# Four-layer kernel, last phase: finished rows stored to the output at once, spline parts placed by three engines and added there by accumulating transfers

## The reference, cut to what matters

```
tile_idx = argmax over the tiles of the chosen cluster
x_slice = xf[token, the 8 features of tile_idx]
tile_min, tile_max = min, max of x_slice over all tokens with that tile
u  = clip((x_slice - mn) / (mx - mn + 1e-08), 0.0, 1.0 - 1e-06)
gi = clip((u * GRID).astype(int32), 0, GRID - 1)
delta = (bases[tile,j,gi] + slopes[tile,j,gi] * (u - gi/GRID)*GRID) * output_scale[tile]
out = x + (zeros with delta at the tile's 8 features)
```

## Time and profile before

| | us |
|---|---|
| median of three runs | 7930.12 |
| the profiled execution's own time | 7928.37 |
| span of its trace | 7926.6 |
| core phase's last instruction on DVE ends | 7681.5 |
| first instruction of the chunks on DVE | 7771.65 |
| last DVE instruction | 7921.9 |

### The profile page before, as it was taken

The page is one execution under the profiler, slowest core; times in us unless marked ns, Lnnn a source line. Parts: engine busy times, 40 slices in busy tenths (PEclk is TensorE's granted clock), DMA queues, the critical chain, the costliest instruction groups (busy, mean ns, idle before and its releaser), DMA issues. The chain is left out here.

```text
span 7926.6 us, 217947 instructions
## 1 busy us (share of the span) xinstructions
PE 7123.9 (90%) x74510; PEld 5211.8 (66%) x74510; DVE 6564.5 (83%) x7897; ACT 4860.3 (61%) x11212; POOL 5927.2 (75%) x3528
## 2 busy tenths in 40 slices
PE   8799999999999999999999999899999997888864
PEld 4577777777777777777777777644444443555542
DVE  7799999999999999999999999822322324999976
ACT  7778878878878877878878877611111112555530
POOL 1499999999999999999999999800000002999964
PEclk9999999999999999999999999999999998999975
DMA  5500000000000000000000000022222112333325
GB/s 209 165 0 17 17 0 17 17 0 17 17 0 17 17 0 17 17 0 17 17 0 17 17 0 6 37 83 74 90 82 88 74 64 102 103 102 102 103 90 159
DMA packets 198189, 389.94 MB, mean 49 GB/s; under 512 B 26225, under 2 KB 51889, under 8 KB 186545
## 3 DMA queue, kind: packets, MB, share of 16 engines
q1 hardware_dynamic: 189088, 370.45, 14.0%
q10 hardware_dynamic: 8976, 17.83, 0.6%
HBM read 208.52 MB, written 179.70 MB: 49 GB/s over the span
## 5 line engine op out<-in xcount | busy, mean ns | idle before, releaser
L494 POOL TENSOR_TENSOR scan_hc<-scan_h,scan_cb 128x1024 f32<-128x1024 f32 x2048 | 4776.3, 2367 | 103.4 <-PE scan_y L617 82.2
L659 DVE TENSOR_TENSOR_SCAN scan_h<-scan_a,scan_carry,scan_u 128x512 f32<-128x512 f32 x4096 | 4800.1, 1252 | 16.4 <-PE scan_u L606 8.4
L553 ACT ACTIVATE scan_a<-scan_dt,scan_aneg 128x512 f32<-128x512 f32 x4096 | 2658.2, 708 | 7.4 <-ACT scan_yo L533 7.4
L606 PE MATMUL scan_u<-scan_dg,scan_v 64*128 64x128 f32 x32768 | 2380.9, 285 | 312.7 <-DVE scan_h L659 268.8
L606 PEld LDWEIGHTS scan_u<-scan_dg,scan_v 64*128 64x128 f32 x32768 | 1992.2, 188 | 793.2 <-DVE scan_h L659 555.9
L617 PE MATMUL scan_y<-scan_ident,scan_hc 128*128 128x128 f32 x16408 | 2251.8, 280 | 14.2 <-ACT scan_yo L533 9.8
L617 PEld LDWEIGHTS scan_y<-scan_ident,scan_hc 128*128 128x128 f32 x16408 | 1758.0, 140 | 271.0 <-ACT scan_yo L533 15.7
L524 ACT ACTIVATE scan_dg<-scan_half,scan_bt 128x64 f32<-128x64 f32 x4096 | 1139.2, 341 | 6.0 <-DVE scan_onward L645 5.3
L164 POOL TENSOR_TENSOR mid_r<-mid_ve,mid_half_neg 128x4 f32<-128x4 f32 x32 | 32.4, 1012 | 1267.5 <-DVE mid_ve L132 780.2
L545 ACT ACTIVATE scan_carry<-scan_h,scan_onward 128x4 f32 (+1 forms) x1008 | 302.9, 301 | 934.6 <-DVE scan_h L659 934.4
L871 ACT ACTIVATE mid_rt<-mid_pb 128x512 f32<-128x512 f32 x64 | 38.2, 597 | 610.1 <-PE mid_pb L945 610.1
(11 more groups left out here) (215 smaller groups left out, 6818.0 us busy)
## 6 DMA issues: line engine op xcount, KB each, us to landing
scratch_y<-scan_yo ACTq DMA_DIRECT2D x17, 1024.0 KB, 4.3
pre_x<-in_x SPq DMA_DIRECT2D x16, 1024.0 KB, 5.7
scratch_dt<-pre_dt SPq DMA_DIRECT2D x16, 1024.0 KB, 5.8
scratch_vr<-pre_vr SPq DMA_DIRECT2D x16, 1024.0 KB, 4.7
scan_dt<-scratch_dt SPq DMA_DIRECT2D x16, 1024.0 KB, 5.3
scan_v<-scratch_vr SPq DMA_DIRECT2D x32, 512.0 KB, 7.7
mid_yr<-scratch_y SPq DMA_DIRECT2D x16, 1024.0 KB, 6.9
mid_x<-in_x SPq DMA_DIRECT2D x16, 1024.0 KB, 8.1
```

What stands on the lines that cost most here:

```text
L494: pool.tensor_tensor(hc[:, q].rearrange("p n (r j) -> p n r j", j=P), h[:, q].rearrange("p n (r j) -> p n r j", j=P), cb[:, bass.ds(b * NS ...
L553: ins = act.activation(a[:, q, n, :], dt[:, par, q, :], ACT.Exp, scale=aneg[:, q, bass.ds(m * 2 + n, 1)])
L606: mm = pe.matmul(u_ps[:, q % 2, g, k * HP:(k + 1) * HP, :], v[row, par, k, q, :], dg[row, buf, k], start=True, stop=True)
L659: ins = dve.tensor_tensor_scan(h[:, q, n, :], a[:, q, n, :], u_ps[:, q % 2, :, :, n].rearrange("p g t -> p (g t)"), carry[:, q, bass.ds(m ...
```

## The change

`core_phase` stores its rows straight to the output tensor; `oh` and `xs` stay in on-chip memory (named `choice` and `picked`) for both phases. `final_phase` no longer loads rows. It makes the zero rows with `delta` for 8 tiles (1024 tokens) at a time: GpSimd writes tiles 0 to 2 with one instruction each, ACT tiles 3 to 5 with eight instructions each (one per feature), DVE tiles 6 and 7. GpSimd then issues one transfer of 2 MB with `accum_op=ALU.add`, which adds them to the rows in HBM. There are 8 such batches, in the order 4 to 7, 0 to 3, and two buffers. Besides, the table of values is multiplied with the scale once, the 128 x 8704 comparison and its difference go and a rounding gives the cell, the limits of the first half of the tokens come by products on PE, the turning uses PE's transpose, and half of the penalties comes from ACT.

```diff
-                sp.dma_start(x3_s[bass.ds((m + par * (L // P)) * P, P), :], xo[:, par]).then_inc(x3_out[par], 16)
+                sp.dma_start(rows_out[bass.ds((m + par * (L // P)) * P, P), :], xo[:, par]).then_inc(x3_out[par], 16)
             pipelined(sp, ITEMS, [(5, load_decays), (3, load_rows), (1, store)])
-            routed.wait_all(sp, ITEMS - 1)
-            sp.dma_start(oh_out, oh[:]).then_inc(final, 16)
-            sp.dma_start(xs_out, xs[:]).then_inc(final, 16)
-            sp.wait_ge(final, 32)
...
+        add = sb("add", [P, 2, BT, D])
...
+
+        def place(eng, k, i):
+            t = ORDER[k] * BT + i
+            return eng.tensor_tensor(add[:, k % 2, i].rearrange("p (n e) -> p n e", e=SL), oh[:, t, :].rearrange("p (n e) -> p n e", e=1).broadcast_to([P, NT, SL]),
+                                     delta[:, t:t + 1, :].broadcast_to([P, NT, SL]), ALU.mult)
...
+            for dst, src in ((ident, ident_d), (table, table_d), (scale, scale_d), (grid, grid_d)):
...
-
-                sp.wait_ge(out[par], (half + 1) * 16)
-                sp.dma_start(x[:, par], xv[c]).then_inc(x_in[par], 16)
-
-            def store(c, par, half):
-
-                summed.wait_all(sp, c)
-                sp.dma_start(ov[c], x[:, par]).then_inc(out[par], 16)
-            skewed(sp, NCH, [(1, load), (0, store)])
-            for par in range(2):
-                sp.wait_ge(out[par], 16 * (NCH // 2 + 1))
...
-                summed.wait_freed(pool, c)
-                for j in range(J):
-                    last = pool.tensor_tensor(add[:, par, j].rearrange("p (n e) -> p n e", e=SL), oh[:, bass.ds(c * J + j, 1), :].rearrange("p o (n e) -> p (o n) e", e=1).broadcast_to([P, NT, SL]),
-                                              delta[:, par, j:j + 1, :].broadcast_to([P, NT, SL]), ALU.mult)
-                placed.inc(last)
-            in_turn(pool, NCH, place)
+            def send(k):
+                pool.wait_ge(by_pool, k + 1)
+                pool.wait_ge(by_act, k + 1)
+                pool.wait_ge(by_dve, k + 1)
+                pool.dma_start(rows_out[:, ORDER[k] * BT:(ORDER[k] + 1) * BT, :], add[:, k % 2], accum_op=ALU.add).then_inc(added[k % 2], 16)
+            for k in range(NB):
+                pool.wait_ge(delta_made, k + 1)
+                if k > 1:
+                    pool.wait_ge(added[k % 2], 16 * (k // 2))
+                for i in range(BY_POOL):
+                    last = place(pool, k, i)
+                last.then_inc(by_pool, 1)
+                if k:
+                    send(k - 1)
+            send(NB - 1)
+            for b in range(2):
+                pool.wait_ge(added[b], 16 * (NB // 2))
...
+            dve.tensor_scalar(pen[:, 0:HALF], oh[:, 0:HALF], 2.0 * BIG, -BIG, ALU.mult, ALU.add).then_inc(steps, 1)
+            dve.tensor_reduce(best[:, 0, :], xs[:], AX.X, ALU.max).then_inc(steps, 1)
...
+            dve.wait_ge(pen_half, 1)
             for e in range(2):
...
+                link(dve.tensor_tensor(pr[:], pen[:], best[:, e, :].rearrange("p (t o) -> p t o", o=1).broadcast_to([P, TILES, NT]), ALU.min))
...
+                if e == 0:
+                    dve.wait_ge(consts, 64)
+                    dve.tensor_scalar(table[:], table[:], scale[:, 0:1], None, ALU.mult).then_inc(table_ready, 1)
+            dve.wait_ge(ext_turned, 1)
+            dve.tensor_reduce(limt[:], ext_ps, AX.X, ALU.max).then_inc(limt_made, 1)
+            late = slice(HALF, TILES)
             dve.wait_ge(ext_all, 1)
...
-                link(dve.tensor_tensor(pr[:], oh[:], exta[:, e:e + 1, :].broadcast_to([P, TILES, NT]), ALU.mult))
-                link(dve.tensor_reduce(lim[:, e, :], pr[:], AX.X, ALU.add))
...
-            link(dve.tensor_tensor(ge[:].rearrange("p t e g -> p (t e) g"), flat(u16).rearrange("p (t o) -> p t o", o=1).broadcast_to([P, TILES * SL, GRID + 1]),
...
-            link(dve.tensor_tensor(hot[:].rearrange("p t e g -> p (t e) g"), g3[:, :, 0:GRID], g3[:, :, 1:GRID + 1], ALU.subtract))
-            link(dve.tensor_reduce(flat(gi), g3[:, :, 1:GRID], AX.X, ALU.add))
...
-                                             hot[:, bass.ds(c * J + j, 1)].rearrange("p o e g -> p o (e g)").broadcast_to([P, 2, SL * GRID]), ALU.mult)
...
-                dve.wait_ge(x_in[par], (half + 1) * 16)
-                summed.inc(dve.tensor_tensor(x[:, par], x[:, par], add[:, par], ALU.add))
...
+                link(dve.tensor_tensor(pr[:, late], oh[:, late], exta[:, e:e + 1, :].broadcast_to([P, HALF, NT]), ALU.mult))
+                link(dve.tensor_reduce(lim[:, late, e], pr[:, late], AX.X, ALU.add))
...
+                link(dve.tensor_scalar(u16[:, t], u[:, t], float(GRID), None, ALU.mult))
+                link(dve.tensor_scalar(near[:, t], u16[:, t], ROUND, None, ALU.add))
+                link(dve.tensor_scalar(near[:, t], near[:, t], ROUND, None, ALU.subtract))
+                link(dve.tensor_tensor(over[:, t], near[:, t], u16[:, t], ALU.is_gt))
+                link(dve.tensor_tensor(gi[:, t], near[:, t], over[:, t], ALU.subtract))
...
+            def splines(k):
...
+                link(dve.tensor_tensor(hot[:], gi[:, t].rearrange("p t (e o) -> p (t e) o", o=1).broadcast_to([P, BT * SL, GRID]),
...
+                for c in range(2):
...
+                    dve.wait_ge(rows_found, 2 * k + c + 1)
+                    dve.tensor_tensor(wv[:, j], rows_ps[:, c], hot[:, c * J * SL:(c + 1) * J * SL].rearrange("p (t k e) g -> p t k (e g)", k=1, e=SL).broadcast_to([P, J, 2, W]), ALU.mult).then_inc(rows_used, 1)
+                dve.wait_ge(rows_used, 2 * k + 2)
+                link(dve.tensor_reduce(bs[:].rearrange("p t k e -> p (t k e)"), wv[:].rearrange("p t k (e g) -> p (t k e) g", g=GRID), AX.X, ALU.add))
...
+                link(dve.tensor_tensor(d, bs[:, :, 1, :], u16[:, t], ALU.mult))
+                dve.tensor_tensor(d, d, bs[:, :, 0, :], ALU.add).then_inc(delta_made, 1)
+                dve.wait_ge(delta_made, k + 1)
+                if k > 1:
+                    dve.wait_ge(added[k % 2], 16 * (k // 2))
+                for i in range(BY_ACT, BT):
+                    last = place(dve, k, i)
+                last.then_inc(by_dve, 1)
+
+            units(1)
+            for k in range(NB):
+                if k == 2:
+                    dve.wait_ge(limits_found, 1)
+                    link(dve.tensor_copy(lim[:, 0:HALF], limits_ps))
+                    units(0)
+                splines(k)
...
+            act.activation(pen[:, HALF:TILES], oh[:, HALF:TILES], ACT.Identity, bias=-BIG, scale=2.0 * BIG).then_inc(pen_half, 1)
...
+                act.wait_ge(turned, c + 1)
+                act.copy(oht[:, c * J:(c + 1) * J], turn_ps[0:NT, c % 2]).then_inc(turn_copied, 1)
+            for k in range(NB):
+                act.wait_ge(delta_made, k + 1)
+                if k > 1:
+                    act.wait_ge(added[k % 2], 16 * (k // 2))
+                for i in range(BY_POOL, BY_ACT):
+                    t = ORDER[k] * BT + i
+                    for e in range(SL):
+                        last = act.activation(add[:, k % 2, i].rearrange("p (n e) -> p n e", e=SL)[:, :, e], oh[:, t, :], ACT.Identity, scale=delta[:, t, e:e + 1])
+                last.then_inc(by_act, 1)
...
+            pe.wait_ge(consts, 64)
+            for c in range(TILES // J):
+                if c > 1:
+                    pe.wait_ge(turn_copied, c - 1)
                 for j in range(J):
...
+                    mm = pe.transpose(turn_ps[0:NT, c % 2, j, :], oh[:, c * J + j, :], ident[:])
+                mm.then_inc(turned, 1)
+
+            def tables(k, c):
+                if k:
+                    pe.wait_ge(rows_used, 2 * k + c - 1)
...
+                    mm = pe.matmul(rows_ps[:, c, j].rearrange("p k w -> p (k w)"), oht[:, ORDER[k] * BT + c * J + j, :], table[:], start=True, stop=True)
+                mm.then_inc(rows_found, 1)
+
+            pe.wait_ge(turn_copied, TILES // J)
+            pe.wait_ge(table_ready, 1)
+            for c in range(2):
+                tables(0, c)
+            pe.wait_ge(ext_made, 2)
+            for e in range(2):
+                mm = pe.transpose(ext_ps[:, e, :], ext[:, e, :], ident[:])
+            mm.then_inc(ext_turned, 1)
+            pe.wait_ge(limt_made, 1)
+            for i in range(HALF):
+                mm = pe.matmul(limits_ps[:, i, :], oht[:, i, :], limt[:], start=True, stop=True)
+            mm.then_inc(limits_found, 1)
+            for k in range(1, NB):
+                for c in range(2):
+                    tables(k, c)
...
-    xs_s = scratch("xs", [P, N // P, D // NT])
+    out_rows = out.rearrange("b l d -> (b l) d")
...
-    core_phase(nc, D, HEADS, L, a_s, k_s, r_s, vv_s, x2_s, wo, gamma, beta, slopes, key_row, sub_mask, head_mask, ident, x3_s, oh_s, xs_s)
...
+    with nc.sbuf_tensor("choice", [P, N // P, NT], F32) as oh, nc.sbuf_tensor("picked", [P, N // P, D // NT], F32) as xs:
```

(32 more changed lines are left out.)

132 lines of the change are left out of this document (50 added, 82 removed).

## The result

The changed kernel takes 7881.66 us (median; 7877.55 to 7887.19) against 7929.34 before: ratio 0.9943, with an interval of 0.9931 to 0.9956, or 47.7 us less. The forecast was 7892, 38.2 less, within a range of 7848 to 7955. One of its five executions was in the slow state (15108 us, mean granted clock 0.528) and stands in no comparison. The profiled execution took 7881.66 with a span of 7879.9; that is 46.7 under the profiled one of before (7928.37), so the forecast was short by 8.5 there and by 9.5 between the medians.

What follows compares the result with a forecast made beforehand. Chunks were taken as bound by transfers in turn with their waits, not an engine. New end: 7743.3 + 6 x (D + 4.6) + D + (D - 2.5) = 7888.4 at D = 15, 38.2 under before; time 7892, range 7848 to 7955.

Steps and rivals of the forecast that it cites:

- First issue: POOL issues transfer 0 at 7743.3: batch 1's deltas on DVE at 7739.0, then 4.3 of placing.
- the wait for the turned extremes: In the stage over all tokens, DVE waits for PE's transposes and lookups until 7710.3, idling 5.7 us.
- Six periods: Transfers cannot overlap until the last; each period is D + 4.6 (placing 4.3, waits and issue 0.3), six times.
- Tail of two transfers: Only transfers 6 and 7 are both in flight: D + (D - 2.5), 2.5 us credited from the last one's fixed part.
- D: Issue to landing of one 2 MB accumulating transfer: taken as 15 us, bounds 7.3 to 27.3.
- The batch on three engines: Per batch: DVE 8.2 us, ACT 24 activations at 0.341 = 8.2, POOL three tiles at 1.443 = 4.3.
- Rival 1: Accumulating transfers: the add costs no more than a copy, D = 7.3, time 7830; chance 0.16 (D below 12).
- Rival 3: POOL's software writes descriptors before data moves; were that 5 us, D = 20, time 7932; chance 0.12.
- Rival 2: Transfers slow, read, read and write in turn or 2 KB rows held back: D = 27.3, time 7990; chance 0.20.
- Rival 4: Placing: ACT's strided writes cost more than 0.341, the bound only over 0.8 each; no chance of its own.

Runs made afterwards that it cites:

- e8: Changed kernel with all eight tiles of a batch placed by GpSimd, none by ACT and DVE: 7909.93 us, 28 over the changed kernel.
- e2: Changed kernel with plain transfers from GpSimd's queue instead of accumulating ones: 7834.28 us, 47.4 under the changed kernel.
- e6: Changed kernel with GpSimd issuing each transfer behind its own batch's placing, not the next batch's; two buffers: 7823.82 us, 57.8 under the changed kernel.
- e5: Changed kernel with accumulating transfers undone: SP loads and stores rows of 8 tiles, DVE adds the placed parts: 7852.40 us, 29 under the changed kernel.

## Why the prediction was right, and what was off in it

The forecast was right in sign and time, and in its mechanism but for one wait. Its formula splits the end into three, which can be set against the trace:

- **First issue**: forecast 7743.3, measured 7736.75, 6.6 earlier. Of this, 3.0 is DVE's start: 2.7 by earlier phases, in which the change only stores the rows elsewhere, 0.3 by the barrier. **The mis-sized term is the wait for the turned extremes**: forecast 5.7 from the last extreme (in which a small reduction is counted) to the limits, measured 7702.71 - 7701.42 = 1.3, of which 0.95 is the wait; 4.4 less. In the other direction, the second batch took DVE 9.4 and not 8.2, by its contention with POOL: 1.2. The remaining stages come to 0.4 less.
- **Six periods**: forecast 6 x 19.6 = 117.6, measured 117.9.
- **Tail of two transfers**: forecast 27.5 (D + D - 2.5), measured from 7854.69 to 7879.9, 25.2.

The three differ by -6.6, +0.3 and -2.3, together the 8.5.

*The wait on PE.* The forecast had PE start at 7686.6 and end its lookups at 7709.0, behind DVE's extremes. PE started at 7682.53, since the constants were there sooner, and ended them at 7698.77, 2.6 us ahead of the extremes; what is left of the wait is the turning itself. The larger part of the 4.4 us is the clock. The forecast took 0.50 from the earlier trace rows, a stretch of chunks in which PE ran in spurts, busy for 34 of 50 us, at the 1.2 GHz level. Here PE had run the transposes since 7682.53, and the window 7690 to 7700 shows it busy for 7.75 of 10 us at 1.00, the 2.4 GHz level. A busy share alone doesn't tell the two apart; the clock of one stretch should not have been carried to another with only a bound as cover. The transposes took 11.86 / 16 = 0.74 per four and not 0.93, and the eight lookups (16 instructions) 3.72 and not 7.5. At 0.50 four transposes followed one another at 0.87 (from 7684.26 to 7687.72), and the next eight lookups took 7.19; an estimate from these: had the clock stayed at 0.50, PE would have ended near 7704, and DVE would have waited about 3 us more. The lower bound that the prediction gave, nothing if the clock rises, was the case that came.

*The batch on three engines.* Each price was off; all but POOL's placing lie under D and did not matter. ACT's 24 narrow activations took 5.90, 0.246 each and not 0.341. DVE's two placings took 2.17 where the earlier trace rows gave 2 x 0.69, and the next `hot` 2.09 for 1.23; POOL's three tiles took 5.05, not 4.3. Both are slowed by running side by side (e8: POOL alone 1.03 a tile). As the period held only POOL's 5.05 + 0.1 beside D = 14.5, the sum 19.66 agrees with the forecast's 15 + 4.6 because D was 0.5 lower and the placing 0.5 dearer. That the period came out to 0.1 us was luck: two errors of the same size cancelled.

*D.* The forecast chose 15 near "the reads double the time per byte", 1.2 + 12.3, and 1.5 for the start. The windows show the same total in other parts: some 3.3 for the start, 0.7 for the landing and 10.5 for the bytes. The time per byte was doubled, but from a plain transfer of 386 GB/s, not of the 342 that the slope of SP's smaller stores gave. The Trainium skill, "Collectives: The Full Stack", section "The bandwidth ceiling: the fold count and why AG ≠ RS ≠ AR", has such an add run at half the rate of a copy. These runs agree, 194 GB/s against 386 with one transfer under way and 208 against 378 with more (e2, window 7817 to 7828). The landing times, 14.5 against 7.7, stand in nearly the same ratio. The second read, by which the Trainium skill explains it, no run here shows.

*The tail.* The last two transfers were in flight together, without a pause of the DMA engines between them. The forecast took 2.5 us off for that; it was 3.8 (2 x 14.5 - 25.2).

**The rivals.** Rival 1, the add costs no more than a copy, fell: 14.5 against 7.7. Its price was sound, 7830 against the 7834.28 of e2, which is what it described. Rival 3, descriptors in front, fell in size: the issue keeps POOL for 1.57 us, and with a quarter of the packets for 1.20; a plain transfer by the same software lands in 7.7. A start of about 3.3 us, against 1.5 of the plain one, is what is left of it. Rival 2, slow transfers, fell: D stayed under the 19.8 from which it decides. Rival 4 had no ground: ACT was cheaper than assumed.

**What the prediction did not see.** It took the transfers' turn for a property of the change and asked only whether period times eight eats the gain of the front. It does not, but the placing of the issue behind the next batch's wait costs 57.8 us (e6), more than the whole gain of 47.7. Relative to before, e5 with the new front, the new placing and a plain load and sum gives 75 us; the accumulation in its given order takes 29 back; sent at once it gives 29 more than e5.

## What to carry to other kernels

With two buffers, issue a batch's transfer ahead of anything that waits for the other buffer; if the issue stands behind that wait in the queue, the second buffer buys nothing, and the period is landing time plus fill time. Engines that are all under half busy beside a DMA share under 1 (0.72 here) are a sign of it: look for who may issue while a transfer is under way, before making either faster. An accumulating transfer took about twice the landing time of a plain one here; weigh it against a load and an add on an engine. In this kernel it won only when its transfers overlapped.

To see what a landing time is made of, cut one transfer into windows. An average over a stretch in which the data have already run out reads as a lower pace: e2 shows 378 GB/s from 7817 to 7828 and 302 from 7820 to 7830.

## What the runs showed of the hardware

- An accumulating transfer of SBUF rows into HBM, issued by POOL: 14.5 us for 2 MB, 9.5 for 1 MB, 13.1 for 2 MB in long pieces; 194 GB/s in the middle of one, 207 to 208 with several in flight. The plain one: 7.7 us, 386 GB/s in the middle of one, 378 with two in flight. Its issue takes 1.57 on POOL, the plain one's 0.93, SP's 0.38. The first of a phase took 15.6 and 1.84.
- DVE and POOL slow each other on tensor-tensor work in SBUF. DVE: 1.23 alone, 2.09 beside POOL, for 128x1024. POOL: a tile of 128x512 takes 1.03 alone, 1.68 beside short DVE work, and 2.75 (8.25 / 3) beside a DVE sum of 128x4096, which itself takes 5.28 there and 4.43 alone.
- A strided activation of 128x64 with a scale per partition runs at a distance of 0.246 us.
- PE's granted clock rose to 1.00 within the row of transposes and stayed there through the lookups. It was still 1.00 at 7701, after a pause of 2.7 us (7698.77 to 7701.47), and fell to 0.50 in the next pause, ahead of the small products (two columns each), which kept PE busy without a gap for 13.8 us and did not bring it back:

```profile
7701.00:7702.00 1.00, 0.41 (x2) 0.14 (x2) 0.38 (x2) 0.00 (x0) 0.45 (x1) 1.00 0.00 0
7702.00:7703.00 1.00, 0.16 (x1) 0.17 (x1) 0.64 (x2) 0.00 (x0) 0.28 (x1) 0.52 0.00 0
7706.00:7710.00 4.00, 4.00 (x20) 4.00 (x20) 3.93 (x3) 0.00 (x0) 0.00 (x0) 0.50 0.00 0
```
